# Folding a head's running maximum to 256 columns on VectorE before TensorE turns it

## The chip, the cores and the metric

The kernel runs on one core of one Trainium2 chip. The metric is the device time of one execution in microseconds. Its engines are TensorE (PE in the rows; PEld its weight loads), VectorE (DVE), ScalarE (ACT), GpSimd (POOL) and SyncE (SP), which issues the transfers.

## What is computed

The reference is a decoder layer over x (4 batches, 256 rows, 512 columns) in three parts, each followed by a layer norm: causal self-attention with 32 heads of 16, cross-attention with 32 query heads of 128 over 1601 context rows, and a feed-forward part with 28 experts of low rank. The change lies in the cross-attention:

```python
B, L, Lk = 4, 256, 1601; NHEAD, NKV, HDIM = 32, 8, 128; G = NHEAD // NKV
q = (query @ Wq + bq).reshape(B, L, NKV, G, HDIM)
k_, v_ = jnp.split(kv @ Wkv + bkv, 2, axis=-1)
k = k_.reshape(B, Lk, NKV, HDIM)
v = v_.reshape(B, Lk, NKV, HDIM)
scores = jnp.einsum('blkgd,bmkd->bkglm', q, k) * scale
attn = jax.nn.softmax(scores, axis=-1)
o = jnp.einsum('bkglm,bmkd->blkgd', attn, v).reshape(B, L, NHEAD * HDIM)
return o @ Wo + bo
```

The softmax takes the maximum over the 1601 keys of each query away first. That maximum is what the change is about.

## The kernel before

The batches run one after the other, in each the 32 heads of the cross-attention, 128 heads in all. Scores lie turned: keys on the 128 partitions, the 256 queries of a head along the columns. A head's 1601 keys make 13 tiles of 128 (the last of 65), and two tiles make one slot of 512 columns, tile 2s in columns 0 to 255 and tile 2s+1 in 256 to 511: seven slots (NSL), the last with one tile only.

Each engine runs through one list of slots (SLOTS). The constants SCORE, SHIFT, EXP, LOW and VALUE say by how many slots a step of a head lies ahead of its products with the values; MAX_TURN, MAX_COL and MAX_ROW do so for the steps of the maximum. So three heads are under way at a time. Between them run jobs (run_job on TensorE, job_high on ScalarE, job_low on VectorE), the projections that make keys (K), values (V) and queries (Q) of later heads and the output (O) of earlier ones. Which job stands in which slot is a fixed table. Products of fp32 accuracy are made of three products of high and low parts (kh and kl, qh and ql, vh and vl, ph and pl).

The way of a head's maximum:
- scores (TensorE) fills sbank, two banks in turn; keep_scores (ScalarE) copies it to kept_s.
- maximum (VectorE) folds slot after slot into mxa, 128 partitions by 512 columns, the running maximum; the last slot touches 65 partitions and 256 columns only (line 928).
- turn_maxima (TensorE, line 1220) turns mxa, four squares of 128x128, into the bank mbank, so that queries lie on partitions.
- row_maxima (VectorE, line 938) reduces each query's 256 numbers there to one, mcol.
- spread_maxima (TensorE, line 1228) turns mcol, broadcast, back to rows, and keep_max (ScalarE, line 729) copies it to mrow.
- shift_scores (GpSimd, line 534) subtracts mrow from kept_s; exponentials (ScalarE) makes ph and pbank from it, low_and_sum (VectorE) makes pl (line 949) and the running sum sua (line 957), and weigh (TensorE) multiplies with the values into dn.

Behind it fold_sums (GpSimd, line 542) adds the halves of sua, sum_rows, row_reciprocals (line 964) and spread_reciprocals (line 1307) make the reciprocals, normalize (VectorE, line 971) multiplies, and finish_head (GpSimd, from line 553) adds the bias and splits the result. In batch 0 GpSimd's split_weight (lines 524 and 526) also splits the weights for all batches.

The engines wait for each other by semaphores. mx_ok counts the steps of maximum, tm_mm the turns, mc_ok the reductions, mr_mm the spreads. In the slot in which the last maximum of a head stands, VectorE's list is: low parts and sums, normalize of an earlier head, the last maximum; the next slot begins with a job's low part (ql of a query job, line 909). In the self-attention VectorE adds qr from t1 and t2, both in SBUF (line 832), while GpSimd takes the context's low parts (line 515).

Of the kernel before, what the change touches and what calls it, by code (L numbers as in the profile page):

```python
# [32 lines left out]
ALU = mybir.AluOpType  # L33
ACT = mybir.ActivationFunctionType
AX = mybir.AxisListType

P = 128
B, S, D = 4, 256, 512
DC = D // P
TB = S // P  # L40
# [29 lines left out]
NSL = (KT + 1) // 2  # L70
# [54 lines left out]
def chunk_of(s):  # L125

    return min(min(LK, 2 * P * (s + 1)) - 1, LK - 2) // KCH[0][1]
# [57 lines left out]
def build(nc, x, x_t, ctx_t, ws, wso, wk_in, wv_in, wq_in, wo_in, bo_s, bo_x, wb, wga, wlb, rope, consts, wk2, wv2, wq2, wo2, out, nb=B):  # L185
    with ExitStack() as ctx:
        def sb(name, shape, dt=F32, stack=ctx):
            return stack.enter_context(nc.sbuf_tensor(name, shape, dt))

        def sem(name):  # L190
            return ctx.enter_context(nc.semaphore(name))
# [19 lines left out]
        ident = cst[:, C_ID:C_ID + P]  # L211
# [57 lines left out]
        mxa = sb("mxa", [P, 2 * S])  # L269
        sua = sb("sua", [P, 2 * S])  # L270
        suc = sb("suc", [P, S])
        mcol = sb("mcol", [P, TB])
# [8 lines left out]
        sbank, pbank, mbank = [bank[2][:, :], sp4[:, 0, :]], [sp4[:, 1, :], sp4[:, 2, :]], sp4[:, 3, :]  # L281
# [19 lines left out]
        sc_mm, cp_ok, mx_ok, tm_mm, mc_ok, mr_mm, mr_ok = (sem(n) for n in ("sc_mm", "cp_ok", "mx_ok", "tm_mm", "mc_ok", "mr_mm", "mr_ok"))  # L301
# [11 lines left out]
        def ring(b, *job_):  # L313
            return b * NJ + JOB_AT[job_]
# [472 lines left out]
        def _(dve):  # L787
# [22 lines left out]
            for b in range(nb):  # L810
# [60 lines left out]
                for u in range(NQ):  # L871
                    m, e = divmod(u, 2)
# [43 lines left out]
                def maximum(h, s):  # L916

                    n = b * NHB + h
                    k, cols = n * NSL + s, S * len(KEYS[s])
                    dve.wait_ge(cp_ok, k + 1)  # L920
                    if s == 1:
                        dve.wait_ge(tm_mm, n)
                        last = kept_s[:, n % 2, 0:2, :].rearrange("p t q -> p (t q)")
                    else:
                        dve.wait_ge(mx_ok, n * (NSL - 1) + s - 1)
                        last = mxa[:, 0:cols]
                    if s == NSL - 1:
                        nc.vector.tensor_tensor(mxa[0:LAST, 0:cols], sbank[k % 2][0:LAST, 0:cols], mxa[0:LAST, 0:cols],
                                                ALU.max).then_inc(mx_ok, 1)
                    else:  # L930
                        nc.vector.tensor_tensor(mxa[:, 0:cols], sbank[k % 2][:, 0:cols], last, ALU.max).then_inc(mx_ok, 1)

                def row_maxima(h):

                    n = b * NHB + h
                    dve.wait_ge(tm_mm, n + 1)
                    dve.wait_ge(mr_mm, n)
                    nc.vector.tensor_reduce(mcol[:, :], mbank.rearrange("p (a n) -> p a n", a=TB), AX.X, ALU.max).then_inc(mc_ok, 1)  # L938

                def low_and_sum(h, s):  # L940

# [109 lines left out]
        def _(pe):  # L1051
# [15 lines left out]
            for b in range(nb):  # L1067
# [87 lines left out]
                for u in range(NQ):  # L1155
                    m, e = divmod(u, 2)
# [35 lines left out]
                def scores(h, s):  # L1192

                    n = b * NHB + h
                    p = h // NHD
                    k = n * NSL + s
                    if k >= 2:
                        a, z = divmod(k - 2, NSL)
                        pe.wait_ge(cp_ok, k - 1)
                        pe.wait_ge(mx_ok, a * (NSL - 1) + z)  # L1200
                    pe.wait_ge(freed, ring(b, "Q", p, h % NHD) + RING + 1)
                    if h % G == 0:
                        pe.wait_ge(freed, ring(b, "K", p, h % NHD // G * len(KCH) + chunk_of(s)) + RING + 1)
                    for e, (i, w) in enumerate(KEYS[s]):
                        dst, keys = sbank[k % 2][0:w, e * S:(e + 1) * S], slice(i * P, i * P + w)
                        mm(dst, kh[:, keys], qh[:, h % QH, :], True, False)
                        mm(dst, kh[:, keys], ql[:, h % QH, :], False, False)
                        last = mm(dst, kl[:, keys], qh[:, h % QH, :], False, True)
                    last.then_inc(sc_mm, 1)

                def turn_maxima(h):

                    n = b * NHB + h
                    pe.wait_ge(mx_ok, (n + 1) * (NSL - 1))
                    if n >= 2:
                        pe.wait_ge(nm_ok, n - 1)
                    for tb in range(TB):
                        for e in range(2):
                            col = (2 * tb + e) * P
                            last = nc.tensor.transpose(mbank[:, col:col + P], mxa[:, e * S + tb * P:e * S + (tb + 1) * P], ident)  # L1220
                    last.then_inc(tm_mm, 1)

                def spread_maxima(h):
# [111 lines left out]
                for tb in range(TB):  # L1335
                    rows = slice(tb * P, (tb + 1) * P)
                    for c in range(DC):
                        last = mm(mx[:, tb, 0:GA], xt[:, c, rows], wgat[:, c, :], c == 0, c == DC - 1)
                    last.then_inc(f_mm, 1)
                for tb in range(TB):  # L1340
                    for c in range(DC):
                        last = mm(bank[tb][:, :], xt[:, c, tb * P:(tb + 1) * P], wbt[:, c, :], c == 0, False)
                last.then_inc(f_base, 1)
                pe.wait_ge(f_v, at(b, N_FV, N_FV))
                for tb in range(TB):
                    for k, n in enumerate((P, ER - P)):
                        last = nc.tensor.transpose(pv[0:n, tb, k * P:(k + 1) * P], hg[:, tb, k * P:k * P + n], ident)
# [81 lines left out]
```

## Time and the profile before

| | us |
|---|---|
| median of 3 runs | 2933.26 |
| lowest and highest of them | 2927.9, 2936.42 |
| time of the profiled execution | 2936.57 |
| its span in the profile | 2934.8 |
| TensorE busy | 2736.7 |
| VectorE busy | 2034.5 |
| ScalarE busy | 1958.7 |
| GpSimd busy | 1649.8 |

The span is what the profiler saw from the first to the last instruction; 1.8 us lie around it. Busy times are sums of instruction records, and records of one engine can overlap: a matmul's record begins when it starts and ends when its result is written, while the next one has long begun. TensorE's granted clock has a mean of 0.976 of full speed over the span.

### The profile page before, as it was taken

What the parts mean: (1) busy time and instruction counts of PE and PEld (TensorE: products, weight loads), DVE (VectorE), ACT (ScalarE), POOL (GpSimd) and SP (SyncE); (2) the same over time, 40 slices, a digit from 0 to 9 for tenths busy, and PEclk for the clock granted to TensorE, in tenths of its full rate; (3) what the DMA queues carried; (4) which work ended last, traced back from release to release, by engine and by line L of the source; (5) the groups of instructions that cost most, each with busy time, mean ns of one, the idle gap of its engine ahead of it and who ended that gap; (6) DMA issues with size and microseconds to landing.
All of it is one profiled execution on the core that took longest, in us unless ns stands there. A gap on an engine that the chain in (4) does not pass through costs nothing.

```text
span 2934.8 us, 60869 instructions
## 1 busy us (share of the span) xinstructions
PE 2736.7 (93%) x20784; PEld 2522.8 (86%) x20784; DVE 2034.5 (69%) x4012; ACT 1958.7 (67%) x4168; POOL 1649.8 (56%) x1678
## 2 busy tenths in 40 slices
PE   6899999999889999999889999999988999999996
PEld 4688989998569999999757999999966899999995
DVE  2367777778447877787744877777765587878785
ACT  3476676767457767676655877777756576767674
POOL 3279798957215656565711656555652265656563
PEclk8899999999999999999999999999989999999998
DMA  5446565612421212121231112212133121212113
GB/s 170 148 147 213 179 209 180 209 66 73 150 61 40 99 44 102 44 102 44 101 129 46 61 70 74 71 66 80 66 126 95 42 87 44 99 46 95 51 46 110
DMA packets 97920, 285.13 MB, mean 97 GB/s; under 512 B 9936, under 2 KB 18256, under 8 KB 94416
## 3 DMA queue, kind: packets, MB, share of 16 engines
q1 hardware_dynamic: 97616, 281.24, 28.2%
q8 instruction: 171, 2.80, 0.4%
q14 instruction: 133, 1.09, 0.1%
HBM read 237.16 MB, written 44.04 MB: 96 GB/s over the span
## 4 chain that ended last, share of the span: by engine, by line
PE 68%; issue 11%; POOL 9%; ACT 6%; DVE 4%; DMA 2%; DVEq 0%; POOLq 0%; ACTq 0%; SPq 0%
PE bank L1058 39%; PE dn L1058 13%; PE sp L1058 10%; POOL kept_s L534 4%; ACT ph L739 2%; PE bank L1124 2%; PE sp L1220 1%; POOL orw L553 1%; PE sp L1228 1%; POOL ol L557 1%; PE sp L1307 1%; DVE mcol L938 1%; ACT sp L744 1%; POOL hib L524 1%; POOL lob L526 1%
## 5 line engine op out<-in xcount | busy, mean ns | idle before, releaser
L534 POOL TENSOR_TENSOR kept_s<-kept_s,mrow 128x512 f32<-128x512 f32 (+1 forms) x896 | 1063.1, 1218 | 595.4 <-ACT mrow L729 595.2
L949 DVE TENSOR_TENSOR pl<-sp,ph 128x512 fp32r<-128x512 f32 (+1 forms) x896 | 577.8, 645 | 81.0 <-ACT sp L744 77.5
L739 ACT ACTIVATE ph<-kept_s 128x512 fp32r<-128x512 f32 (+1 forms) x896 | 534.0, 596 | 47.1 <-POOL kept_s L534 44.1
L744 ACT ACTIVATE sp<-kept_s 128x512 f32<-128x512 f32 (+1 forms) x896 | 506.0, 565 | 2.4 <-DVE sua L957 2.4
L1058 PE MATMUL dn<-ph,vh 128*128 128x256 f32 (+1 forms) x1664 | 489.8, 294 | 2.2 <-DVE pl L949 1.3
L1058 PE MATMUL dn<-ph,vl 128*128 128x256 f32 (+1 forms) x1664 | 472.1, 284 | 0.0
L1058 PE MATMUL dn<-pl,vh 128*128 128x256 f32 (+1 forms) x1664 | 471.5, 283 | 0.0
L957 DVE TENSOR_TENSOR sua<-sp,sua 128x512 f32<-128x512 f32 (+1 forms) x640 | 401.0, 627 | 0.0
L721 ACT ACTIVATE kept_s<-bank 128x512 f32<-128x512 f32 x384 | 228.6, 595 | 232.8 <-PE bank L1058 232.2
L721 ACT ACTIVATE kept_s<-sp 128x512 f32<-128x512 f32 x384 | 228.7, 595 | 192.9 <-PE sp L1058 192.6
L1058 PEld LDWEIGHTS dn<-ph,vh 128*128 128x128 f32 (+1 forms) x1664 | 317.2, 191 | 10.3 <-DVE pl L949 3.2
L1058 PEld LDWEIGHTS dn<-pl,vh 128*128 128x128 f32 (+1 forms) x1664 | 317.0, 191 | 4.1
L1058 PEld LDWEIGHTS dn<-ph,vl 128*128 128x128 f32 (+1 forms) x1664 | 317.2, 191 | 0.0
L1058 PE MATMUL bank<-wvx,ctxh 128*128 128x256 f32 (+1 forms) x1664 | 306.5, 282 | 2.5 <-DVE vl L913 2.0
L1058 PE MATMUL bank<-ctxh,wk 128*128 128x400 f32 (+1 forms) x1024 | 290.5, 346 | 3.1 <-DVE xres L888 3.1
L1058 PEld LDWEIGHTS bank<-wvx,ctxh 128*128 128x128 f32 (+1 forms) x1664 | 250.9, 184 | 6.2 <-DVE vl L913 6.2
L1058 PE MATMUL bank<-qh,kh 128*128 128x256 f32 (+1 forms) x832 | 242.2, 291 | 5.2 <-DVE ql L909 5.2
L553 POOL TENSOR_SCALAR orw<-orw,cst 128x256 f32<-128x256 f32 x128 | 118.7, 927 | 218.4 <-DVE orw L971 218.4
L1058 PE MATMUL sp<-qh,kh 128*128 128x256 f32 (+1 forms) x832 | 237.3, 285 | 0.0
L1058 PE MATMUL bank<-wvx,ctxl 128*128 128x256 f32 (+1 forms) x832 | 233.7, 281 | 0.0
L1058 PE MATMUL bank<-ql,kh 128*128 128x256 f32 (+1 forms) x832 | 232.9, 280 | 0.0
L1058 PE MATMUL bank<-qh,kl 128*128 128x256 f32 (+1 forms) x832 | 232.8, 280 | 0.0
(144 smaller groups left out, 6671.9 us busy)
## 6 DMA issues: line engine op xcount, KB each, us to landing
wqx<-wq SPq DMA_DIRECT2D x128, 512.0 KB, 3.3
wox<-wo SPq DMA_DIRECT2D x64, 1024.0 KB, 4.9
wk<-wk SPq DMA_DIRECT2D x32, 512.0 KB, 3.3
wvx<-wv SPq DMA_DIRECT2D x16, 1024.0 KB, 6.2
raw<-in_ctx_t SPq DMA_DIRECT2D x48, 200.0 KB, 2.5
wqk<-in_ws SPq DMA_DIRECT2D x17, 513.0 KB, 4.4
raw<-in_wq_in SPq DMA_DIRECT2D x32, 256.0 KB, 4.0
wq<-hib SPq DMA_DIRECT2D x32, 256.0 KB, 2.0
```

Source lines behind the costliest of these rows:

```text
L524: nc.gpsimd.tensor_copy(hib[:, :], raw[:, r % 2, :]).then_inc(w_hi, 1)
L526: nc.gpsimd.tensor_tensor(lob[:, :], raw[:, r % 2, :], hib[:, :], ALU.subtract).then_inc(raw_free, 1)
L534: nc.gpsimd.tensor_tensor(kept_s[:, n % 2, i:z, :], kept_s[:, n % 2, i:z, :], mrow[:, n % 2, :].unsqueeze(1).broadcast_to([P, z - i, S]), ...
L553: nc.gpsimd.tensor_scalar(o, o, bias, None, ALU.add).then_inc(oh_ok, 1)
L557: nc.gpsimd.tensor_tensor(ol[:, n % 4, :], o, oh[:, n % 4, :], ALU.subtract).then_inc(ot_ok, 1)
L721: nc.scalar.activation(dst, src[:, :], ACT.Copy).then_inc(cp_ok, 1)
L739: nc.scalar.activation(ph[:, k % PH, 0:cols], src, ACT.Exp, scale=XSCALE).then_inc(ph_ok, 1)
L744: nc.scalar.activation(pbank[k % 2][:, 0:cols], src, ACT.Exp, scale=XSCALE).then_inc(pr_ok, 1)
L949: nc.vector.tensor_tensor(pl[:, k % PH, 0:cols], src, ph[:, k % PH, 0:cols], ALU.subtract).then_inc(pl_ok, 1)
L957: nc.vector.tensor_tensor(sua[:, 0:cols], src, sua[:, 0:cols], ALU.add).then_inc(su_ok, 1)
L1058: return nc.tensor.matmul(dst, lhs, rhs, start=first, stop=final)
L1124: last = nc.tensor.transpose(s_turn[:, z:z + P], pn[:, n % PNR, a:a + P], ident)
```

## The change

VectorE takes the maximum of mxa's two halves behind the last step of maximum, so that the running maximum has 256 columns. TensorE turns two squares of it in place of four, and the reduction reads 256 columns of mbank in place of 512. The counts of mx_ok grow from six to seven for each head; TensorE's turn waits for the seventh.

```diff
@@ maximum(h, s), VectorE
-                        dve.wait_ge(mx_ok, n * (NSL - 1) + s - 1)
+                        dve.wait_ge(mx_ok, n * NSL + s - 1)
                         last = mxa[:, 0:cols]
...
+                    if s == NSL - 1:
+                        dve.wait_ge(mx_ok, n * NSL + s)
+                        nc.vector.tensor_tensor(mxa[:, 0:S], mxa[:, 0:S], mxa[:, S:2 * S], ALU.max).then_inc(mx_ok, 1)
@@ row_maxima(h), VectorE
-                    nc.vector.tensor_reduce(mcol[:, :], mbank.rearrange("p (a n) -> p a n", a=TB), AX.X, ALU.max).then_inc(mc_ok, 1)
+                    nc.vector.tensor_reduce(mcol[:, :], mbank[:, 0:S].rearrange("p (a n) -> p a n", a=TB), AX.X, ALU.max).then_inc(mc_ok, 1)
@@ scores(h, s), TensorE
-                        pe.wait_ge(mx_ok, a * (NSL - 1) + z)
+                        pe.wait_ge(mx_ok, a * NSL + z - (1 if a and z == 0 else 0))
@@ turn_maxima(h), TensorE
-                    pe.wait_ge(mx_ok, (n + 1) * (NSL - 1))
+                    pe.wait_ge(mx_ok, (n + 1) * NSL)
                     if n >= 2:
                         pe.wait_ge(nm_ok, n - 1)
                     for tb in range(TB):
-                        for e in range(2):
-                            col = (2 * tb + e) * P
-                            last = nc.tensor.transpose(mbank[:, col:col + P], mxa[:, e * S + tb * P:e * S + (tb + 1) * P], ident)
+                        last = nc.tensor.transpose(mbank[:, tb * P:(tb + 1) * P], mxa[:, tb * P:(tb + 1) * P], ident)
```

VectorE's order before, in batch 1, head 22, from the sums ahead of the last maximum to the reduction (orw is the normalization of an earlier head, mxa the last maximum, ql the low part of a query job, mcol the reduction):

```order
L957 TENSOR_TENSOR sua<-sp,sua 128x512
L971 TENSOR_TENSOR orw<-sp,orw 128x256
L928 TENSOR_TENSOR mxa<-bank,mxa 65x256
L909 SCALAR_TENSOR_TENSOR ql<-bank,cst,qh 128x256
L949 TENSOR_TENSOR pl<-sp,ph 128x512
L957 TENSOR_TENSOR sua<-sp,sua 128x512
L949 TENSOR_TENSOR pl<-sp,ph 128x512
L957 TENSOR_TENSOR sua<-sp,sua 128x512
L938 TENSOR_REDUCE mcol<-sp 128x2
```

The same place of VectorE's order with the change (lines behind the new ones count three more):

```order
L960 TENSOR_TENSOR sua<-sp,sua 128x512
L974 TENSOR_TENSOR orw<-sp,orw 128x256
L928 TENSOR_TENSOR mxa<-bank,mxa 65x256
L934 TENSOR_TENSOR mxa<-mxa 128x256
L909 SCALAR_TENSOR_TENSOR ql<-bank,cst,qh 128x256
L952 TENSOR_TENSOR pl<-sp,ph 128x512
L960 TENSOR_TENSOR sua<-sp,sua 128x512
L952 TENSOR_TENSOR pl<-sp,ph 128x512
L960 TENSOR_TENSOR sua<-sp,sua 128x512
L941 TENSOR_REDUCE mcol<-sp 128x2
```

One instruction is new, the fold at line 934, directly behind the last maximum; all that stood behind it now stands behind the fold.

TensorE's order before at the same head's turn (dn takes the values of an earlier head, bank the scores of the next):

```order
L1058 MATMUL dn<-pl,vh 128x256
L1058 MATMUL dn<-ph,vl 128x256
L1220 MATMUL sp<-cst,mxa 128x128 x4
L1058 MATMUL bank<-qh,kh 128x256
L1058 MATMUL bank<-ql,kh 128x256
```

And with the change:

```order
L1061 MATMUL dn<-pl,vh 128x256
L1061 MATMUL dn<-ph,vl 128x256
L1221 MATMUL sp<-cst,mxa 128x128 x2
L1061 MATMUL bank<-qh,kh 128x256
L1061 MATMUL bank<-ql,kh 128x256
```

The turn stands where it stood and has two transposes in place of four.

## Rows read from the trace of the kernel before

**Rows 1.** The page, span, and busy time, share and instructions of each engine.

```profile
span 2934.8 us, 60869 instructions
...
PE 2736.7 (93%) x20784; PEld 2522.8 (86%) x20784; DVE 2034.5 (69%) x4012; ACT 1958.7 (67%) x4168; POOL 1649.8 (56%) x1678
```

**Rows 2.** The page, the chain that ended last, shares by engine.

```profile
PE 68%; issue 11%; POOL 9%; ACT 6%; DVE 4%; DMA 2%; DVEq 0%; POOLq 0%; ACTq 0%; SPq 0%
```

**Rows 3.** The waits: waiting line, releaser, total us, times, longest.

```profile
POOL kept_s L534 <- ACT mrow L729: 595.2, 114, 26.3
...
PE sp L1228 <- DVE mcol L938: 26.8, 60, 1.6
```

**Rows 4.** TensorE in time, batch 1, head 22: start, us, instruction, idle before.

```profile
1281.64 0.60 PE L1220 MATMUL sp<-cst,mxa 128*128 128x128 f32 x4
1281.99 0.36 PE L1058 MATMUL bank<-qh,kh 128*128 128x256 f32 x1
...
1284.07 0.28 PE L1058 MATMUL sp<-qh,kl 128*128 128x256 f32 x1
1284.70 0.43 PE L1228 MATMUL sp<-cst,mcol 128*128 128x128 f32 x2 [0.35 <-DVE mcol L938]
1284.89 0.36 PE L1058 MATMUL dn<-ph,vh 128*128 128x256 f32 x1
```

**Rows 5.** VectorE in time, the same head.

```profile
1280.07 0.41 DVE L928 TENSOR_TENSOR mxa<-bank,mxa 65x256 f32<-65x256 f32 x1
1280.40 0.47 DVE L909 SCALAR_TENSOR_TENSOR ql<-bank,cst,qh 128x256 fp32r<-128x256 f32 x1
...
1282.76 0.69 DVE L949 TENSOR_TENSOR pl<-sp,ph 128x512 fp32r<-128x512 f32 x1 [0.69 <-ACT sp L744]
...
1283.97 0.68 DVE L938 TENSOR_REDUCE mcol<-sp 128x2 f32<-128x512 f32 x1
```

**Rows 6.** GpSimd in time, the same head.

```profile
1280.26 0.93 POOL L553 TENSOR_SCALAR orw<-orw,cst 128x256 f32<-128x256 f32 x1 [1.08 <-DVE orw L971]
```

**Rows 7.** VectorE's groups by form: count, busy us, mean ns, idle before.

```profile
L938 DVE TENSOR_REDUCE mcol<-sp 128x2 f32<-128x512 f32 x128 | 87.1, 680 | 0.0
...
L854 DVE TENSOR_REDUCE nmx<-sp 128x1 f32<-128x256 f32 x128 | 53.0, 414 | 0.0
```

**Rows 8.** Dense heads in time: first turn of 12; the last head.

```profile
169.89 0.66 PE L1220 MATMUL sp<-cst,mxa 128*128 128x128 f32 x4
...
2875.02 0.41 DVE L928 TENSOR_TENSOR mxa<-sp,mxa 65x256 f32<-65x256 f32 x1
...
2875.49 0.66 PE L1220 MATMUL sp<-cst,mxa 128*128 128x128 f32 x4 [0.32 <-DVE mxa L928]
...
2877.74 0.68 DVE L938 TENSOR_REDUCE mcol<-sp 128x2 f32<-128x512 f32 x1
```

**Rows 9.** VectorE in time, two places in batch 0's self-attention.

```profile
34.48 0.71 DVE L832 TENSOR_TENSOR qr<-t 128x256 f32<-128x256 f32 x1
...
85.70 0.84 DVE L832 TENSOR_TENSOR qr<-t 128x256 f32<-128x256 f32 x1
```

**Rows 10.** GpSimd in time at the same two places.

```profile
33.88 1.04 POOL L515 TENSOR_TENSOR ctxl<-raw,ctxh 128x400 fp32r<-128x400 f32 x1 [1.28 <-ACT ctxh L603]
...
85.22 1.03 POOL L515 TENSOR_TENSOR ctxl<-raw,ctxh 128x400 fp32r<-128x400 f32 x1 [1.41 <-ACT ctxh L603]
```

**Rows 11.** All of line 832: count, duration in ns (least, median, most).

```profile
L832 DVE TENSOR_TENSOR qr<-t x16: 414/416/840, 18.9 to 2261.3; 128x256 f32<-128x256 f32 x16
```

**Rows 12.** GpSimd in time, weight splits beside a maximum: first and last of five.

```profile
183.75 1.29 POOL L526 TENSOR_TENSOR lob<-raw,hib 128x512 fp32r<-128x512 f32 x1
...
545.20 1.29 POOL L526 TENSOR_TENSOR lob<-raw,hib 128x512 fp32r<-128x512 f32 x1
```

**Rows 13.** VectorE in time at these two heads.

```profile
183.32 0.41 DVE L928 TENSOR_TENSOR mxa<-bank,mxa 65x256 f32<-65x256 f32 x1
...
186.77 0.68 DVE L938 TENSOR_REDUCE mcol<-sp 128x2 f32<-128x512 f32 x1
...
544.78 0.41 DVE L928 TENSOR_TENSOR mxa<-sp,mxa 65x256 f32<-65x256 f32 x1
```

## The prediction

> **What bounds the kernel now.** I read the page's busy line first, then the chain, the waits, and last the instructions of single heads in order of time. TensorE is busy 93% of a span of 2934.8 us, VectorE 69%, GpSimd 56% [rows 1], and the chain that ended last runs 68% of the time over TensorE [rows 2]. So what leaves TensorE's queue is worth close to its full time, where TensorE doesn't wait for others in the same stretch.
>
> It does wait at one place that the change touches. In 60 of the 128 heads TensorE stands idle in front of the transposes that spread the row maxima (spread_maxima), until VectorE's reduction of the turned maxima is done, 26.8 us in all [rows 3]. In the other 68 heads no such wait is recorded, so there TensorE sets the pace.
>
> One steady head shows the loop. TensorE turns the four squares at 1281.64, goes on with scores and values, starts its last product at 1284.07 and then waits 0.35 us for the reduction [rows 4]. VectorE ends the last maximum at 1280.48, works through ql, pl and sua, waits 0.69 us for ScalarE's exponentials, and starts the reduction at 1283.97 for 0.68 us [rows 5]. The wait at 1282.76 hangs on scores that TensorE computed ahead of the turn: so the time of the spread is set by a chain that does not pass through the turn. There a shorter reduction pays, a shorter turn doesn't; in the 68 other heads it is the other way round.
>
> **The change, part by part.**
>
> *Two transposes fewer.* Each lasts some 0.27 us by the records, but they overlap; what counts is the distance of the starts. From the first of four transposes to the product behind them it is 1281.99 - 1281.64 = 0.35 us; from the first of two, in the spread, 1284.89 - 1284.70 = 0.19 us [rows 4]. So the turn gets 0.17 us shorter (I take 0.17 for 0.16 to 0.18). In 68 heads: 68 x 0.17 = 11.6 us off. The Trainium skill, "TensorE: Matmul & The Clock Gate", Part 4 on transposes, gives about 275 ns for a 128x128 transpose in one kernel's context. By that price the same 68 heads would give back 68 x 0.55 = 37 us; the rows agree with it as a duration and not as a cost, since the starts lie 0.09 us apart.
>
> *A reduction of 256 columns for 512.* Now 680 ns for 512 columns; the same kind of reduction over 256 columns from the same memory takes 414 ns [rows 7]: 0.27 us less, at the end of the chain that TensorE waits for. Bounds: nothing (were the time fixed) and 0.34 (half).
>
> *The fold.* 128x256 plus 128x256 on VectorE. A sum of 256 columns with both inputs in SBUF takes 416 ns at the median [rows 11], of which the next instruction hides 0.08 (one start 0.33 after the other) [rows 5]. It waits for the maximum in front of it, so it can't start 0.08 us before that one's end, but some 0.04 behind it (my estimate): VectorE is 0.41 + 0.04 = 0.45 us later behind it. Queued behind it are ql, pl, sua, and then the pl that now waits 0.69 us for ScalarE [rows 5]: 0.45 lies inside 0.69, so in steady heads the reduction starts as early as before. The turn waits for the fold too: 1281.64 is 1.16 us behind the maximum's end [rows 4, 5], which covers 0.45, so its cost is nothing here; without that cover TensorE would wait those 0.45 us at the turn.
>
> *Where that cover is missing.* In each batch, three heads (the second and the last two) run dense on VectorE: in the very last, from the maximum at 2875.02 to the reduction at 2877.74 no idle time is recorded, and the turn at 2875.49 starts 0.06 us behind the maximum's end, for which it had waited. Such turns last 0.66 us and not 0.60 (first and last of the 12 in the rows) [rows 8]. There the reduction ends 0.45 - 0.27 = 0.18 us later, and TensorE, which waits for it, with it: 12 x 0.18 = 2.2 us on.
>
> So without any disturbance: 48 x 0.27 = 13.0 and 68 x 0.17 = 11.6 off, 2.2 on: -22.4 us.
>
> *GpSimd in the way.* The fold is the first instruction of this phase of VectorE that reads both inputs from SBUF, while GpSimd works beside it. The trace has the same form in batch 0's self-attention: qr<-t (two inputs in SBUF) takes 0.41 at the median but 0.84 at most [rows 11]. It took 0.84 and 0.71 us just where a GpSimd instruction was under way, from 85.22 to 86.25 and from 33.88 to 34.92 [rows 9, 10]. It ended at 86.54 and 35.19, that is 0.29 and 0.27 behind GpSimd's end: it stood still until GpSimd was done and then streamed its 256 columns. The Trainium skill states such a rule in "SBUF — State Buffer", Who interferes with whom: a VectorE instruction with two SBUF inputs and a GpSimd one that reads SBUF lock each other out for a whole instruction. By that rule, the trace agrees.
>
> In a steady head the fold would start at 1280.52. But GpSimd's bias addition, released by the normalization ahead of the maximum, runs from 1280.26 for 0.93 us [rows 6]. The fold then ends at 1281.19 + 0.28 = 1281.47 and not at 1280.93: 0.54 us more. The three instructions behind it (0.47, 0.68 and 0.68 us, each less the 0.08 that the next one hides) end their slots at 1281.39 + 1.59 = 1282.98, and the waiting pl starts 0.2 late. The reduction's end gains 0.07 in such a head instead of 0.27; in heads where VectorE's idle time is longer it still gains 0.27. I take 0.2 as the mean over those 43 heads that no weight piece hits: 3 us of gain lost. In the 12 dense heads the delay isn't covered; between 0 and 0.54 each I take 0.4: 5 us lost. In batch 0 GpSimd also splits weights: in five heads with a waiting spread (first and last in the rows) a 1.29 us subtraction starts at 183.75 and 545.20, while the maximum ends at 183.73 and 545.19, so that both want the port within 0.04 us of each other [rows 12, 13]. If GpSimd is first the fold ends at 183.75 + 1.29 + 0.28 = 185.32 instead of 184.18, 1.14 late. Up to the reduction at 186.77 the queue works 3.13 of 3.45 us (one start 0.33, one 0.40, four 0.60), so the reduction starts 0.45 + 1.14 - 0.32 = 1.27 late: that is the cost in each of the five, 6 us in all; I take half, 3. Sum: -22.4 + 3 + 5 + 3 = -11.4 us, and -8 to -14 for the race's two ends.
>
> The profiled execution took 2936.6 us, 3 us above the median of 2933.26, inside the spread of the runs. I apply the difference to the median: 2933.3 - 11.4 = 2922 us. A difference of 0.3% (9 us) is what this kernel's measurement can tell from none.
>
> **Rivals.**
>
> *No lock at the fold* (20%). The lock is seen here against GpSimd subtractions and sums of two tensors; the bias addition takes one tensor and a scalar, and its 0.93 us may hold the port for a part only. Then nearly the full sum: 2933.3 - 22.4 = 2911 us.
>
> *Given back later* (15%). TensorE's next stops are the reciprocals' spread and pl. If these were bound by something that doesn't move with the spread, the gain would end there as a longer wait: 2933 us, within 0.3%. Against it: GpSimd's shift waits 595.2 us for the row of maxima [rows 3], which comes from the spread, so what follows is tied to it and moves with it.
>
> *Slower: VectorE's queue sets the turn and the spread in all waiting heads* (10%). If the lock costs 0.54 everywhere and VectorE has no idle time to hide it, the reduction comes 0.45 + 0.54 - 0.27 = 0.72 later in 60 heads: +43 - 11.6 = +32 us, 2965 us. It decides from the point at which the idle time between maximum and reduction falls below 0.72 us; it is 0.69 in the head shown, so the half-way case (0.1 lost in each) is near, while a full loss needs dense queues such as only 12 heads show [rows 5, 8].
>
> **How the numbers follow.** The case with the lock, partly hidden (-5 to -17 us), 55%; about two thirds of it lies beyond 9 us. Faster: 0.37 + 0.20 + 0.01 = 0.6 roughly; same: 0.18 + 0.13, 0.3; slower: 0.1. Range: 2908 (no lock, 0.02 more for each transpose pair) to 2931 (the gain almost given back), which leaves out the slow case and part of the second rival.
>
> **What the profile after would show.** The turn as two transposes with the next product some 0.19 us behind the first; the reduction at about 414 ns; 26.8 us of waits at the spread falling where the fold is hidden, with starts of the spread 0.2 to 0.27 earlier than the scores ahead suggest. For the lock: folds with a median well over 0.41 us, near 0.9, and each ending 0.28 behind the end of a GpSimd instruction; in batch 0 some of 1.5. Without it all folds take 0.41. The head period of the late steady heads (15.4 us) should shrink by 0.1 to 0.27, of the dense last head grow by 0.2 to 0.7. Wrong would be: a turn that waits for the fold in steady heads, or waits at the spread as long as before with head periods unchanged.

## The result, and the profile after

The changed kernel takes 2913.92 us at the median (2911.8 to 2919.37, 5 runs), the kernel before 2933.26 on the same chip. The ratio is 0.9943 with an interval of 0.9928 to 0.9957: 16.7 us faster, between 13 and 21. Measured again on another chip (experiment e10), the same kernel gave 0.9961, 0.9948 to 0.9973. The profiled execution took 2911.9 us for a span of 2910.1.

The page's head and its chain, to be read beside [rows 1, 2]:

```profile
span 2910.1 us, 60485 instructions
...
PE 2707.1 (93%) x20528; PEld 2495.1 (86%) x20528; DVE 2076.5 (71%) x4140; ACT 1956.8 (67%) x4168; POOL 1654.4 (57%) x1678
...
PE 59%; ACT 5%; issue 5%; DVE 4%; POOL 3%; DMA 1%; DVEq 0%; ACTq 0%; POOLq 0%; SPq 0%
```

256 matmul instructions less (two for each of 128 heads), 128 VectorE instructions more. TensorE is as busy in share as before: what was taken from its queue came off the span. The waits of TensorE and GpSimd, beside [rows 3]:

```profile
POOL kept_s L534 <- ACT mrow L729: 574.5, 114, 26.1
...
PE sp L1229 <- DVE mcol L941: 24.2, 60, 1.6
...
PE sp L1221 <- DVE mxa L934: 12.0, 19, 1.3
```

The wait at the spread is nearly as long as before, in the same 60 heads. That does not say that the shorter reduction brought nothing: a wait is an idle time of TensorE, and TensorE now comes to it earlier too. The third row is new: in 19 heads the turn stands and waits for the fold. Before, it waited for the last maximum in the last head of each batch alone, 1.3 us in all. VectorE's groups by form, beside [rows 7]:

```profile
L934 DVE TENSOR_TENSOR mxa<-mxa 128x256 f32<-128x256 f32 x128 | 82.2, 642 | 4.5
...
L941 DVE TENSOR_REDUCE mcol<-sp 128x2 f32<-128x256 f32 x128 | 52.8, 413 | 0.0
```

The reduction came out at the expected length. The fold's mean of 642 ns is half as much again as the 425 ns that it takes with no GpSimd instruction beside it, so something holds it. One steady head of batch 1 in time, TensorE first, then VectorE, then GpSimd, to be read beside [rows 4 to 6]:

```profile
1273.10 0.38 PE L1221 MATMUL sp<-cst,mxa 128*128 128x128 f32 x2
1273.24 0.36 PE L1061 MATMUL bank<-qh,kh 128*128 128x256 f32 x1
...
1275.90 0.43 PE L1229 MATMUL sp<-cst,mcol 128*128 128x128 f32 x2 [0.30 <-DVE mcol L941]
1276.09 0.36 PE L1061 MATMUL dn<-ph,vh 128*128 128x256 f32 x1
```

```profile
1271.54 0.41 DVE L928 TENSOR_TENSOR mxa<-bank,mxa 65x256 f32<-65x256 f32 x1
1271.98 0.49 DVE L934 TENSOR_TENSOR mxa<-mxa 128x256 f32<-128x256 f32 x1
1272.39 0.47 DVE L909 SCALAR_TENSOR_TENSOR ql<-bank,cst,qh 128x256 fp32r<-128x256 f32 x1
...
1274.23 0.69 DVE L952 TENSOR_TENSOR pl<-sp,ph 128x512 fp32r<-128x512 f32 x1 [0.17 <-ACT sp L744]
1274.83 0.68 DVE L960 TENSOR_TENSOR sua<-sp,sua 128x512 f32<-128x512 f32 x1
1275.43 0.41 DVE L941 TENSOR_REDUCE mcol<-sp 128x2 f32<-128x256 f32 x1
```

```profile
1271.72 0.92 POOL L553 TENSOR_SCALAR orw<-orw,cst 128x256 f32<-128x256 f32 x1 [1.08 <-DVE orw L974]
```

Three things are to be seen. The turn stands 0.14 us ahead of the next product, before it was 0.35. The fold starts 0.03 behind the end of the last maximum, with GpSimd's bias addition under way from 1271.72 to 1272.64; it takes 0.49 us and is done at 1272.47, 0.17 ahead of GpSimd's end. And the pl that waits for ScalarE now waits 0.17 us in place of 0.69: the fold went into that idle time.

A head of batch 0 in time, GpSimd, VectorE and TensorE, beside [rows 12, 13]:

```profile
183.45 1.28 POOL L526 TENSOR_TENSOR lob<-raw,hib 128x512 fp32r<-128x512 f32 x1
184.69 1.47 POOL L534 TENSOR_TENSOR kept_s<-kept_s,mrow 128x512 f32<-128x512 f32 x1
```

```profile
183.47 1.55 DVE L934 TENSOR_TENSOR mxa<-mxa 128x256 f32<-128x256 f32 x1
```

```profile
185.07 0.44 PE L1221 MATMUL sp<-cst,mxa 128*128 128x128 f32 x2 [0.79 <-DVE mxa L934]
185.26 0.37 PE L1061 MATMUL bank<-qh,kh 128*128 128x256 f32 x1
```

Here the partner subtracts two tensors and started 0.02 us ahead. The fold takes 1.55 us and ends at 185.02, 0.29 behind the subtraction's end, and TensorE waits 0.79 us for it.

All 128 folds of this trace fall into three kinds. 82 stand beside the bias addition and take 0.48 to 0.49 us. 39 stand beside an instruction of GpSimd that reads two tensors, 18 weight splits and 21 shifts, and every one of these ends 0.28 to 0.29 us behind that instruction's end. Seven have no GpSimd instruction beside them and take 0.42 to 0.43 us. In 15 steady heads of batches 1 to 3 the fold takes 0.72 to 0.85 us beside a shift, and their periods are nevertheless those of e1, which has no fold: their pl waited 0.86 us or more before the change.

The head's period is the better ruler for the gain: from one spread's start to the next. Each figure is the difference of two starts in the trace, in us. The steady, key and value rows are heads of batch 1; "all" is from the first spread of a batch to its last.

| | before | after | e1 no fold | e2 fold alone |
|---|---|---|---|---|
| head with key work | 20.80 | 20.53 | 20.53 | 20.80 |
| heads with value work | 19.16, 23.68 | 18.95, 23.44 | the same | 19.16, 23.68 |
| late steady heads | 15.46, 14.05 | 15.20, 13.81 | the same | 15.46, 14.05 |
| second head | 15.73 | 15.94 | 15.48 | 16.20 |
| last head but one | 14.24 | 14.51 | 13.98 | 14.77 |
| last head | 12.43 | 12.91 | 12.16 | 13.15 |
| batch 0, all | 568.69 | 568.21 | 558.48 | 570.74 |
| batch 1, all | 552.44 | 546.32 | 542.96 | 554.14 |
| batch 2, all | 550.91 | 546.36 | 546.17 | 554.20 |
| batch 3, all | 552.34 | 546.26 | 546.13 | 552.68 |

Batches 1 to 3 gained 6.1, 4.6 and 6.1 us, batch 0 only 0.5: 17.2 us together. The two profiled spans lie 24.7 us apart; the other 7.5 us stand outside the batches, most of them between two, where the change touches nothing and where the profiles of all kernels scatter by some us (163 to 167 us from one batch's last spread to the next one's first). The 17.2 us agree with the ratio, but the two traces differ in more than the change. In four heads of each batch TensorE's granted clock falls in some executions from 2.4 to 1.2 GHz for a while, which adds 1.54 us to the head (last section). This happened in five heads of batches 1 to 3 before and in six with the change. Batch 2's 4.6 us hold one such head more; without it each of the three batches gained 6.1. In the profile of e10, the changed kernel again, with five such heads, batches 1 to 3 gained 18.4 us and batch 0 1.4 against the same profile of before. So the change is worth 17 to 20 us inside the batches, and one profile doesn't say it more closely.

### The profile page after: what moved, and what is told of

Read it like the earlier page. It is cut to its first block, busy times and chain, and to the rows that moved or that the text cites. A ratio compares the mean times of both kernels' runs of the same rounds, so it can differ in the third digit from the quotient of the medians.

```text
span 2910.1 us, 60485 instructions
## 1 busy us (share of the span) xinstructions
PE 2707.1 (93%) x20528; PEld 2495.1 (86%) x20528; DVE 2076.5 (71%) x4140; ACT 1956.8 (67%) x4168; POOL 1654.4 (57%) x1678
## 4 chain that ended last, share of the span: by engine, by line
PE 59%; ACT 5%; issue 5%; DVE 4%; POOL 3%; DMA 1%; DVEq 0%; ACTq 0%; POOLq 0%; SPq 0%
PE bank L1061 34%; PE dn L1061 12%; PE sp L1061 9%; ACT ph L739 2%; POOL kept_s L534 2%; PE bank L1127 1%; ACT sp L744 1%; PE sp L1229 1%; DVE sua L960 1%; PE sp L1308 1%; DVE mcol L941 1%; POOL orw L553 1%; ACT kept_s L721 0%; POOL ol L557 0%; PE sp L1221 0%
## 5 line engine op out<-in xcount | busy, mean ns | idle before, releaser
L534 POOL TENSOR_TENSOR kept_s<-kept_s,mrow 128x512 f32<-128x512 f32 (+1 forms) x896 | 1065.4, 1219 | 574.7 <-ACT mrow L729 574.5
```

The lines of the kernel that those rows point to most:

```text
L534: nc.gpsimd.tensor_tensor(kept_s[:, n % 2, i:z, :], kept_s[:, n % 2, i:z, :], mrow[:, n % 2, :].unsqueeze(1).broadcast_to([P, z - i, S]), ...
```

## The experiments

Two explanations stood against each other. One is the prediction's: the fold is held until GpSimd's instruction has ended, whichever it is. The other, early release (E): only a GpSimd instruction on two tensors holds it to its end, while the bias addition, one tensor and a scalar for each partition, lets it go early. Beside them the parts' own prices (fold, turn, reduction) and the places of the loss (dense heads, batch 0) were to be told apart. The edits are against the changed kernel. e1 to e4 were measured together (kernel before: 2933.92 us), then e5 to e8 on the same chip (2934.03), then e9 and e10 on another (2926.8).

**e1: no fold.** Two squares and 256 columns, without the fold and its wait. The odd key tiles are then missing from the maximum that is subtracted; which number is subtracted doesn't change a softmax. The counts of mx_ok go back to six for each head.

```diff
...
-                    if s == NSL - 1:
-                        dve.wait_ge(mx_ok, n * NSL + s)
-                        nc.vector.tensor_tensor(mxa[:, 0:S], mxa[:, 0:S], mxa[:, S:2 * S], ALU.max).then_inc(mx_ok, 1)
...
```

> The fold is left out, and with it the odd key tiles from the maximum that is subtracted (softmax is not changed by which number is subtracted). TensorE turns two squares, VectorE reduces 256 columns. Theory A (savings 0.27 us in the 60 heads in which TensorE waits for the reduction and 0.22 in the 68 others, less some 14 us that the fold costs, half of it in batch 0): -16 - 15 = -31 us, ratio 0.9894, 2902 us; batch 0 gains as much as the others, some 7.8 us from first to last spread. Rival B (the fold is hidden nearly everywhere, the savings are smaller than counted): as the changed kernel, 2914 to 2917 us.

Measured: 2902.38 us, 0.9887 (0.9872 to 0.9902), 33 us less than before. Both savings without their price come to 33 us, or 0.26 a head. By the table every steady, key and value head has the same period with the fold and without it: there it costs nothing. Its price is in the dense heads (0.46, 0.53 and 0.75 us in the three) and in batch 0, which is 9.7 us shorter than in the changed kernel's first profile and 8.8 shorter than in its second (e10).

**e2: the fold alone.** Four squares and the reduction over 512 columns, with the fold ahead of them.

```diff
-                        last = nc.tensor.transpose(mbank[:, tb * P:(tb + 1) * P], mxa[:, tb * P:(tb + 1) * P], ident)
+                        for e in range(2):
+                            col = (2 * tb + e) * P
+                            last = nc.tensor.transpose(mbank[:, col:col + P], mxa[:, e * S + tb * P:e * S + (tb + 1) * P], ident)
...
-                    nc.vector.tensor_reduce(mcol[:, :], mbank[:, 0:S].rearrange("p (a n) -> p a n", a=TB), AX.X, ALU.max).then_inc(mc_ok, 1)
+                    nc.vector.tensor_reduce(mcol[:, :], mbank.rearrange("p (a n) -> p a n", a=TB), AX.X, ALU.max).then_inc(mc_ok, 1)
```

> The fold is done and waited for, but TensorE still turns four squares and VectorE still reduces 512 columns: the fold's price alone. Theory A: +14 us, ratio 1.0047, 2947 us, 7 of it in batch 0, 2 in each other batch (its three dense heads). Rival B: 0 to +4 us.

Measured: 2950.21 us, 1.0057 (1.0043 to 1.0071): 17 us more than before. With e1 the books close: -33 + 17 = -16 against the change's -16.7. The periods show the same picture from the other side: steady heads as before, dense heads 0.47, 0.53 and 0.72 longer. That is 6.9 us in 12 heads; the rest of the 17 isn't found in the profile, whose run is the shortest of the five (2944 to 2954 us). A part of the rest goes with TensorE's granted clock: the profiled run had a mean of 0.977 and a span of 2942.5 us, the four others 0.972 to 0.975 and 2946.3 to 2952.5. Eight runs of the kernel before at 0.977 on that chip have spans of 2930.8 us on the mean, so at the same clock the fold alone costs some 12 us.

**e3: one input of the fold from PSUM.** It reads half of the running maximum and a score bank, so that it has one SBUF input. The other half is left out of the subtracted maximum, and the scores that fill this bank next wait for the fold too.

```diff
-                        nc.vector.tensor_tensor(mxa[:, 0:S], mxa[:, 0:S], mxa[:, S:2 * S], ALU.max).then_inc(mx_ok, 1)
+                        nc.vector.tensor_tensor(mxa[:, 0:S], mxa[:, 0:S], sbank[k % 2][:, 0:S], ALU.max).then_inc(mx_ok, 1)
...
-                        pe.wait_ge(mx_ok, a * NSL + z - (1 if a and z == 0 else 0))
+                        pe.wait_ge(mx_ok, a * NSL + z + (1 if z == NSL - 1 else 0))
```

> The fold's second input is the score bank in PSUM in place of mxa's upper half, of the same size (so the maximum leaves out part of the keys; the scores wait for the fold as well). Theory A (GpSimd's reading of SBUF holds up a fold with two inputs in SBUF): all 128 folds take 0.41 us, none 1.5; only the dense heads pay 0.45 us each, 5 us: -31 + 5 = -26 us, ratio 0.991, 2907 us. Rival C (the long folds of batch 0 come from something else, as a crowded VectorE or SBUF): folds of 1.5 us remain, time as the changed kernel.

Measured: 2913.37 us, 0.9928 (0.9915 to 0.9942). All of line 934: count, then least, median and most in ns:

```profile
L934 DVE TENSOR_TENSOR mxa<-mxa,bank x64: 420/422/423, 151.8 to 2837.7; 128x256 f32<-128x256 f32 x64
...
L934 DVE TENSOR_TENSOR mxa<-mxa,sp x64: 420/422/424, 170.9 to 2850.3; 128x256 f32<-128x256 f32 x64
```

Not one of 128 folds is held, beside the same GpSimd instructions: what holds the fold is bound to its second SBUF input. The last head's period is 12.62 us, so of the 0.75 that the fold costs there, 0.46 is its stream and 0.29 the hold. The time was expected at 2907 us and came 6 above. TensorE's waits for the fold in batch 0 are nearly gone (below, with e6), but the batch still took 567.05 us. One stretch of it shows a part of the reason (start and end, length, busy us of PE, PEld, VectorE, ScalarE, GpSimd, granted clock, DMA share, GB/s), e3 first, then the changed kernel:

```profile
250.00:260.00 10.00, 7.73 (x39) 7.29 (x38) 7.44 (x15) 4.95 (x11) 9.76 (x10) 0.66 0.76 271
```

```profile
250.00:260.00 10.00, 8.86 (x68) 8.03 (x67) 9.39 (x17) 7.45 (x16) 9.92 (x10) 1.00 0.85 307
```

TensorE issues 39 matmuls there for 68, at a mean granted clock of 0.66, so for a part of the stretch at the lower level (1.2 GHz). The fifth to seventh heads of batch 0, in which this stretch lies, take 54.4 us in e3, 54.7 in the kernel before, 52.3 in the changed one and 48.0 in e1; the kernel before has no fold at all. So what these three heads cost in one profile is no price of the fold. What lowers the clock there isn't shown.

**e4: the reduction reads 256 columns twice.** Its old length without the two transposes.

```diff
-                    nc.vector.tensor_reduce(mcol[:, :], mbank[:, 0:S].rearrange("p (a n) -> p a n", a=TB), AX.X, ALU.max).then_inc(mc_ok, 1)
+                    nc.vector.tensor_reduce(mcol[:, :], mbank[:, 0:S].rearrange("p (a n) -> p a n", a=TB).unsqueeze(2).broadcast_to([P, TB, 2, P]), AX.XY, ALU.max).then_inc(mc_ok, 1)
```

> The changed kernel, but the reduction reads its 256 columns twice, 512 in all, as long as before. Theory A: 0.27 us later in the 60 heads in which TensorE waits, +16 us against the changed kernel, ratio to before 0.9995, 2932 us. Rival D (TensorE's two transposes less are the gain, the reduction is off the path): as the changed kernel, 2914 to 2917 us.

Measured: 2930.13 us, 0.999 (0.9981 to 0.9999), so nearly the whole gain is lost again. The reduction's line and TensorE's wait for it:

```profile
L941 DVE TENSOR_REDUCE mcol<-sp x128: 675/681/683, 155.3 to 2865.6; 128x2 f32<-128x512 f32 x128
...
PE sp L1229 <- DVE mcol L941: 41.8, 60, 1.9
```

The wait grows from 24.2 to 41.8 us, 0.29 us in each of the 60 heads, for a reduction 0.27 us longer. In these heads its length counts in full, the length of the turn doesn't. The periods part the two savings: late steady heads are back at 15.44 us and heads with key work at 20.79, as before the change, though their turn has two transposes; heads with value work keep 18.94 and 23.43, as in the changed kernel, though their reduction is long.

**e5: the bias addition on two tensors.** The same sum, with the bias spread out as a second operand.

```diff
-                nc.gpsimd.tensor_scalar(o, o, bias, None, ALU.add).then_inc(oh_ok, 1)
+                nc.gpsimd.tensor_tensor(o, o, bias.broadcast_to([P, S]), ALU.add).then_inc(oh_ok, 1)
```

> The changed kernel with GpSimd's bias addition as a sum of two tensors (the bias broadcast) in place of tensor and scalar. In 82 heads the fold starts 0.27 us behind that instruction's start and took 0.48 us. Theory E (a GpSimd sum of two tensors holds the port to its end, the tensor-and-scalar form lets go halfway): the bias addition takes some 0.74 us and the fold ends 0.28 us behind its end, so it takes 0.75 us; time +0 to +3 us against the changed kernel. Rival F (what matters is how far the GpSimd instruction has come, not its form): the fold still takes 0.48.

Measured: 2914.65 us, 0.9933 (0.9915 to 0.9952), as the changed kernel. The fold and the bias addition:

```profile
L934 DVE TENSOR_TENSOR mxa<-mxa x128: 424/612/1551, 151.3 to 2853.1; 128x256 f32<-128x256 f32 x128
...
L553 POOL TENSOR_TENSOR orw<-orw,cst x128: 602/612/827, 189.0 to 2873.1; 128x256 f32<-128x256 f32 x128
```

This is the cleanest of the tests. The partner is now shorter (0.61 for 0.93 us) and yet the median fold is longer (612 for 486 ns). In one head the addition runs from 1419.14 to 1419.75 and the fold from 1419.42 to 1420.03: it ends 0.28 behind its partner's end, as every fold beside a two-tensor instruction does. So early release is right, and the prediction's rule is right for the form that its rows showed and wrong for the other; the lengths were expected at 0.74 and 0.75 us and came out at 0.61. How long the form with a scalar reads its input, and so why it lets the fold go, no run shows. That the time doesn't move shows what a tenth of a microsecond is worth in a steady head: nothing.

**e6: the fold as a reduction.** One operand, which walks over the halves in pairs, into a tile of its own.

```diff
+        mxf = sb("mxf", [P, S])
...
-                        nc.vector.tensor_tensor(mxa[:, 0:S], mxa[:, 0:S], mxa[:, S:2 * S], ALU.max).then_inc(mx_ok, 1)
+                        nc.vector.tensor_reduce(mxf[:, :], mxa.rearrange("p (t q) -> p q t", t=2), AX.X, ALU.max).then_inc(mx_ok, 1)
...
-                        last = nc.tensor.transpose(mbank[:, tb * P:(tb + 1) * P], mxa[:, tb * P:(tb + 1) * P], ident)
+                        last = nc.tensor.transpose(mbank[:, tb * P:(tb + 1) * P], mxf[:, tb * P:(tb + 1) * P], ident)
```

> The fold as a reduction over pairs, one input from SBUF of 512 columns, into a tile of its own. Theory A: every fold takes 0.68 us, none is held up; batch 0 gains 0.85 us in eight heads, the dense heads of the others lose up to 0.2: 4 us below the changed kernel, ratio to before 0.993, 2911 us. Rival C: folds of 1.5 us and more remain in batch 0.

Measured: 2911.87 us, 0.9923 (0.9907 to 0.9939).

```profile
L935 DVE TENSOR_REDUCE mxf<-mxa x128: 694/706/715, 156.0 to 2851.7; 128x256 f32<-128x512 f32 x128
```

It streams 512 columns and is never held. Steady heads are as fast as with the short fold, dense heads some 0.5 us longer than before (16.21, 14.71, 12.88), and batch 0 takes 561.05 us, 7 less. That is more than the scatter of one profile: three kernels with the held fold, the changed one, e10 and e5, have 568.2, 567.3 and 566.3 us there, two without, e6 and e7, 561.1 and 560.7. TensorE's wait for the fold between 130 and 760 us, in the changed kernel, then in e3, then in e6:

```profile
PE sp L1221 <- DVE mxa L934: 9.1, 11, 1.3
```

```profile
PE sp L1221 <- DVE mxa L934: 1.5, 3, 0.8
```

```profile
PE sp L1222 <- DVE mxf L935: 2.4, 3, 1.1
```

In that stretch the kernel before and e1 have 0.3 us of such a wait, for the last maximum of the last head. So batch 0 pays for held folds at the turn, and either way of not being held takes some 7 us of idle time away.

**e7: reduction in batch 0, the two-input fold elsewhere.**

```diff
...
+                        if b == 0:
+                            nc.vector.tensor_reduce(mxf[:, :], mxa.rearrange("p (t q) -> p q t", t=2), AX.X, ALU.max).then_inc(mx_ok, 1)
+                        else:
+                            nc.vector.tensor_tensor(mxf[:, :], mxa[:, 0:S], mxa[:, S:2 * S], ALU.max).then_inc(mx_ok, 1)
...
```

> The fold as a reduction in batch 0 and as a maximum of two halves in the others, into a tile of its own. Theory A: batch 0 as in the kernel with reductions, the others as in the changed one: 5 us below the changed kernel, ratio 0.9925, 2911 us. Rival: what batch 0 gains is lost in the split of the weights there, 2916 us.

Measured: 2910.72 us, 0.9924 (0.991 to 0.9938). Batch 0 takes 560.65 us, as in e6, and the other three 544.9 to 546.5, with the changed kernel's periods in their dense heads (15.94, 14.50 and 12.92). Against e5, the held version on the same chip, the median is 3.9 us lower, but the intervals of the ratios overlap, so the whole kernel's time doesn't settle these few us; the batch and the waits do.

**e8: the fold one slot early.** The halves are folded before the last key tile, whose maximum then goes over the folded columns: the held instruction sits at another place.

```diff
-                        dve.wait_ge(mx_ok, n * NSL + s - 1)
+                        dve.wait_ge(mx_ok, n * NSL + s - (0 if s == NSL - 1 else 1))
...
-                    if s == NSL - 1:
+                    if s == NSL - 2:
                         dve.wait_ge(mx_ok, n * NSL + s)
                         nc.vector.tensor_tensor(mxa[:, 0:S], mxa[:, 0:S], mxa[:, S:2 * S], ALU.max).then_inc(mx_ok, 1)
...
```

> The fold stands one slot earlier, behind the last but one maximum; the last one works on the folded 256 columns. Theory A: there GpSimd is in its row of shifts, of two tensors each, so most folds take 0.5 to 1.5 us, 0.9 on the mean in all batches; the time is 2914 to 2925 us. Rival G (the place in the queue doesn't matter, only its length): as the changed kernel, folds mostly under 0.5.

Measured: 2915.74 us, 0.9939 (0.9917 to 0.996).

```profile
L934 DVE TENSOR_TENSOR mxa<-mxa x128: 424/656/1553, 153.4 to 2852.8; 128x256 f32<-128x256 f32 x128
```

No turn waits for the fold now (nine, all in dense heads, wait for the last maximum), but its median length rises to 656 ns, for there it more often meets GpSimd's shift, an instruction on two tensors. What one place gained the other lost: in batch 1 a head with value work grew from 23.44 to 23.9 us. It can't be told from the changed kernel.

**e9: no fold in dense heads,** and e7's fold elsewhere. The second and the last two heads of each batch keep four squares and 512 columns.

```diff
+def folds(n):
+
+    return n % NHB not in (1, NHB - 2, NHB - 1)
...
-                    if s == NSL - 1:
+                    if s == NSL - 1 and folds(n):
...
```

> As the mixed fold, but in the second and the last two heads of a batch, where VectorE has no idle time, nothing is folded: TensorE turns four squares and VectorE reduces 512 columns there, as before the change. Theory A: those heads have the periods they had before the change, 0.21, 0.27 and 0.48 us less than in the changed kernel in batches 1 to 3, some 0.5 each in batch 0: 4.6 us below the mixed fold, ratio to before 0.991, 2906 us. Rival H (VectorE's backlog was made up later in the batch anyway): as the mixed fold, 2911 us.

Measured: 2906.24 us, 0.993 (0.9916 to 0.9943), beside e10 on the same chip with 2914.43 us and 0.9961. It lies 8 us below the changed kernel in medians, and the ratios' intervals just don't touch. Since it has e7's fold too, the 8 us aren't the dense heads' alone; by the periods these give some 4 us. Its median is the lowest of all versions whose maximum takes in every key, but e6 and e7, measured on another chip, have ratios of 0.9923 and 0.9924 to its 0.993, so between these three nothing is decided. Its dense heads have the periods of before (15.75, 14.24 and 12.42 us), its batch 0 takes 563.93 us. The last head's turn and spread:

```profile
2846.47 0.66 PE L1238 MATMUL sp<-cst,mxa 128*128 128x128 f32 x4 [0.34 <-DVE mxa L939]
...
2849.46 0.43 PE L1246 MATMUL sp<-cst,mcol 128*128 128x128 f32 x2 [1.62 <-DVE mcol L955]
```

**e10: the changed kernel again,** unedited, as the measure for e9.

> The changed kernel once more, beside the kernel without folds in the dense heads and the kernel before on the same chip. 2914 to 2917 us, ratio 0.9943 within its interval; 17 us between the first and the last spread of the four batches as in its first profile, the rest of the difference changes from run to run.

Measured: 2914.43 us, 0.9961 (0.9948 to 0.9973), span 2913.8. The changed kernel's two medians are the same to 0.5 us, while the kernel before moved from 2933.3 to 2926.8. So a difference of 0.2% between the ratios of kernels that weren't measured side by side says little here. The expected ratio of 0.9943 was missed. From the first to the last spread of the four batches the profile has 19.8 us less than before, where 17 were expected.

## Why the prediction came out as it did

The forecast was faster, 2922 us within 2908 to 2931; it is faster, 2914. By the medians the rival "no lock at the fold", 2911 us, was nearer than the forecast itself; by the ratio, which gives a gain of 16.7 us, forecast (11.4) and rival (22.4) are equally far off. Step by step:

**Two transposes less.** The mechanism is right: where TensorE doesn't wait, their time comes off the head. The size was 0.17 us and is 0.35 - 0.14 = 0.21; the periods of heads with value work shrank by 0.19 to 0.31. The pair had been priced at the spread [rows 4], and that pair stands behind a wait. In the changed kernel the next product starts 0.13 or 0.14 us behind the first transpose in 108 of the 109 turns that don't wait, and 0.19 or 0.20 in 17 of the 19 that do, as at 185.07 above. In 68 heads that is 14 us for 11.6.

**The shorter reduction.** 0.27 us predicted, 0.27 measured, and e4 shows that it counts in full in the waiting heads, and that the turn's length doesn't count there, as the prediction had it.

**The fold is hidden in steady heads.** Right, and by the named cover: pl's wait of 0.69 us [rows 5] shrank to 0.17, and the periods with and without the fold (e1) are equal.

**Dense heads.** The net of +0.18 us plus a hold of 0.4 was to come to 0.58 a head. Measured are 0.21, 0.27 and 0.48, which is 3.8 us in all four batches' 12 heads, if batch 0's are taken like the others', for 7.2. The reasoning (0.45 later, 0.27 given back) holds: the fold's stream costs 0.46 by e3. It is the hold that was mis-sized, taken at 0.4 in each. In batches 1 to 3 the second head's fold has no GpSimd instruction beside it and takes 0.43 us, the last but one's stands beside the bias addition and takes 0.48 to 0.49, and only the last one's is held to the end, by a shift on two tensors:

```profile
2849.73 0.75 POOL L534 TENSOR_TENSOR kept_s<-kept_s,mrow 128x256 f32<-128x256 f32 x1
```

```profile
2850.04 0.73 DVE L934 TENSOR_TENSOR mxa<-mxa 128x256 f32<-128x256 f32 x1
```

**GpSimd in the way of steady heads.** This is the step that failed. The prediction carried a row of a subtraction on two tensors over to the bias addition, which takes one tensor and a scalar, and let the fold end at 1281.47, 0.54 us late. It ends 0.06 late (0.49 for 0.43), before its partner does, in 82 heads. The 3 us for 43 heads are zero, and most of the 5 us for dense heads with them. The sign that the prediction had named for its lock, a median fold near 0.9 us, didn't come: it is 0.486. The Trainium skill, "SBUF — State Buffer", Who interferes with whom, has a VectorE instruction with two SBUF inputs contend with a GpSimd instruction that reads SBUF, and calls the shared ports an exclusive lock. For two-tensor instructions the trace agrees: the fold ends 0.28 to 0.29 us behind GpSimd's end in all 39 of them. For the bias addition in its tensor-and-scalar form it differs, the fold is done 0.17 us ahead of GpSimd's end, and the measurement decides.

**The race in batch 0.** Predicted were five heads that might lose it, 1.27 us each, half taken. In fact twelve folds took over 1.4 us, and in every one GpSimd had started ahead, in eleven by 0.01 to 0.05 us and in one by 0.11. The prediction looked only where the maximum of before ended beside a split in heads with a waiting spread; the splits fall beside the fold in more heads than that, dense ones among them, and there the turn itself waits: the second head of batch 0 takes 16.94 us for 15.73 before. The turn waits in 11 heads of batch 0, and eight of them are steady ones: the prediction had named a turn that waits for the fold in steady heads as a sign of being wrong, and in batch 0 it came. Held for some 1.1 us, the fold ends after the turn's place in TensorE's queue has come up. TensorE's new waits of 9.1 us ate nearly all that batch 0 should have gained.

So the forecast gain was too small by 5 us by the ratio, and this lies in batches 1 to 3, where 10.8 us were forecast. Three quarters of the undisturbed sum of -22.4 us are 16.8 us, and these batches gained 6.1 + 4.6 + 6.1 = 16.8. That the two are equal is luck, since a head at the lower clock more or less moves the second by 1.5: without it, and in e10's profile, the gain is 18.4, a little more than the undisturbed sum, as cheaper turns outweigh dearer dense heads. Batch 0 was to gain 5.6 - 2 - 3 = 0.6 us by the prediction's terms and gained 0.5 (1.4 in e10). This is luck too, for the mechanism is another: the loss is above all the turn's wait in 11 heads, not the spread's in five.

**Given back later** didn't happen: GpSimd's wait for the row of maxima went from 595.2 to 574.5 us, so what follows the spread moved with it. **The slower rival** didn't happen either: in batches 1 to 3 the turn waits for the fold in eight dense heads, 0.22 to 0.52 us each, and in no steady one; batch 0's eight steady heads are all that came of it.

What stays open: why the fold alone (e2) costs 17 us by the medians, some 12 at the same clock, where its profile shows 7 to 8; and what decides in one execution whether a stretch runs at the lower clock. The latter may take a part of the change's own gain: beside each other on one chip, the changed kernel's six runs had mean granted clocks of 0.973 to 0.976, the kernel before's ten 0.976 to 0.980. No run separates the two.

## What to carry to other kernels

An instruction added on an engine with idle time costs nothing in the heads where that idle time stands behind it, and its full length where the queue is dense; so price it by the places, and leave it out of the few dense ones (in e9 their periods are those of before). When another engine's instruction gets in the way, ask for its form before carrying a price over (a row about two tensors said nothing about one tensor and a scalar), and price a short piece of TensorE work by a neighbour that doesn't stand behind a wait.

## What the runs showed of the hardware that was not expected

**One form of GpSimd's instruction hardly holds the fold.** Beside the bias addition with a scalar operand (0.92 us) the fold took 0.48 to 0.49 us, beside the same sum with a tensor operand (0.61 us) it took 0.61, alone 0.43. A fold with one PSUM input took at most 0.424 and a reduction with one SBUF operand at most 0.715, beside the same partners.

**It works both ways.** GpSimd's instruction behind or beside a held fold is longer too: the shift at 184.69 above took 1.47 us and takes 1.29 at the median of all shifts; the bias addition beside a held fold 1.09 to 1.11 in 20 cases, for 0.93.

**The clock after a wait.** In the kernel before, TensorE waits 1.10 us for the reciprocals (line 1307) at 1097.79 and again at 1246.94, with the same work behind. Around them:

```profile
1096.00:1102.00 6.00, 4.90 (x28) 4.54 (x28) 4.51 (x11) 4.02 (x9) 5.93 (x7) 0.72 0.06 10
1247.00:1253.00 6.00, 6.00 (x52) 6.00 (x53) 5.12 (x10) 4.68 (x11) 4.95 (x6) 1.00 0.25 87
```

Behind the first wait the granted clock stands at the lower level (1.2 GHz; 0.52 for the two microseconds from 1098), and 28 matmuls are done for 52; behind the second it stays at 2.4 GHz. A head with the dip is 1.54 us longer than one without. Batches 1 to 3 have 12 such places, with a wait of 1.09 to 1.10 us in each. By the granted clock 5 of them dipped in the kernel before, 6 in the changed one, 3 to 7 in the experiments other than e4. In e4, where the same wait takes 1.02 to 1.05 us, none did. What decides it no run shows. Between two profiles this moves the sum by up to 11 us, as much as many of the differences asked about here. That is why the periods of single heads were compared, and not the spans.
